# A new order of pieces in the third stage of a two-layer decoder

## The reference, cut to what matters

```
x = x + L0_attn(layernorm(x))            # linear attention with convolution and decay
x = x + L0_xattn(layernorm(x), ctx)      # a recurrence with w and u
x = x + L0_ffn(layernorm(x))             # 8 experts, top 2
x = x + L1_attn(layernorm(x))            # D: 16 heads of 16, 4 key heads, rotary, band and sink
x = x + L1_xattn(layernorm(x), ctx)      # E: per token, a 16 x 16 softmax between heads
x = x + L1_ffn(layernorm(x))             # F and M
```

```
mod  = 0.1 * tanh(attn @ A)                       # A: 256 x 16
gate = silu(h @ W_in.T + (mod * (h @ A)) @ B)     # B: 16 x 1024
out  = residual + (gate * (h @ W_up.T)) @ W_down.T
```

## Time and profile before

| | us |
|---|---|
| median of 3 runs (3017.0 to 3025.15) | 3019.28 |
| the profiled execution | 3016.38 |
| its span, first to last instruction | 3014.7 |
| busy PE / DVE / POOL / ACT in the span | 2755.2 / 2487.1 / 2099.5 / 1990.4 |
| the third stage's two costliest lines: POOL L1843 / L1836 | 370.1 / 359.2 |

### The profile page before, as it was taken

The page is one execution under the profiler, slowest core; times in us unless marked ns, Lnnn a source line. Parts: engine busy times, 40 slices in busy tenths (PEclk is TensorE's granted clock), DMA queues, the critical chain, the costliest instruction groups (busy, mean ns, idle before and its releaser), DMA issues. The chain is left out here.

```text
span 3014.7 us, 68300 instructions
## 1 busy us (share of the span) xinstructions
PE 2755.2 (91%) x22096; PEld 2297.8 (76%) x22128; DVE 2487.1 (83%) x5468; ACT 1990.4 (66%) x4233; POOL 2099.5 (70%) x2618
## 2 busy tenths in 40 slices
PE   6999999999999999999799499667899999999988
PEld 3888888888888888888555399535777777777767
DVE  6888888888888888888599677468889898989873
ACT  5888878878787887878576355345566666666642
POOL 6897666666666666666467544379898988898870
PEclk9999999999999999999899699768999999999999
DMA  4555444444434444444344499500000000000000
...
DMA packets 185883, 340.11 MB, mean 113 GB/s; under 512 B 40668, under 2 KB 104037, under 8 KB 178936
## 3 DMA queue, kind: packets, MB, share of 16 engines
...
...
## 5 line engine op out<-in xcount | busy, mean ns | idle before, releaser
L1843 POOL TENSOR_TENSOR l_prod<-l_sco,l_kv 128x256 f32<-128x256 f32 x512 | 370.1, 762 | 35.4 <-DVE l_sco L2350 35.4
L1836 POOL TENSOR_TENSOR l_prod<-l_q,l_kv 128x256 f32<-128x256 f32 x512 | 359.2, 741 | 45.7 <-DVE l_att L2358 45.7
L718 DVE SCALAR_TENSOR_TENSOR a_cq<-a_PQ,a_taps,a_cq 128x504 f32<-128x504 f32 (+2 forms) x384 | 281.9, 734 | 74.9 <-ACT a_cq L584 65.8
L718 DVE SCALAR_TENSOR_TENSOR a_ck<-a_PK,a_taps,a_ck 128x504 f32<-128x504 f32 (+2 forms) x384 | 280.8, 731 | 9.4 <-ACT a_ck L584 0.3
L342 POOL TENSOR_TENSOR a_tq<-a_cq,a_tq 128x512 f32<-128x512 f32 x128 | 166.0, 1297 | 130.7 <-ACT a_tq L590 130.3
L329 POOL TENSOR_TENSOR a_hrs<-a_hve,a_neghalf 128x8 f32<-128x8 f32 x128 | 209.7, 1638 | 25.3 <-DVE a_hve L735 25.3
L485 PE MATMUL a_Y<-a_wo,a_og_parts 128*128 128x256 f32 x1536 | 207.2, 285 | 4.5 <-POOL a_og_parts L336 4.5
L412 PEld LDWEIGHTS a_X<-a_wv,a_xb 128*128 128x128 f32 x1536 | 199.8, 188 | 12.1 <-issue 1.2
L412 PE MATMUL a_PQ<-a_x_hi,a_wqk 128*128 (+1 forms) x512 | 196.1, 424 | 12.6 <-issue 11.9
L342 POOL TENSOR_TENSOR a_tk<-a_ck,a_tk 128x512 f32<-128x512 f32 x128 | 163.6, 1278 | 62.8 <-ACT a_tk L590 62.8
L412 PE MATMUL a_X<-a_wv,a_xb 128*128 128x256 f32 x1536 | 204.1, 282 | 0.8 <-DMA a_xb<-a_x_lo 0.8
...
## 6 DMA issues: line engine op xcount, KB each, us to landing
...
a_dr<-decays SPq DMA_DIRECT2D x256, 64.0 KB, 2.5
...
```

Source lines behind the costliest of these rows:

```text
L718: nc.vector.scalar_tensor_tensor(out=acc, in0=src, scalar=taps[p][:, tap + k:tap + k + 1], in1=acc, op0=ALU.mult, op1=ALU.add).then_inc(s_ ...
L1836: nc.gpsimd.tensor_tensor(out=prod[:, h], in0=qv[:, h:h + 1, :].to_broadcast([P, H, HD]), in1=kk, op=ALU.mult).then_inc(S("E_pqk"), 1)
L1843: nc.gpsimd.tensor_tensor(out=prod[:, h], in0=sco[:, h:h + 1, :].to_broadcast([P, HD, H]), in1=vv, op=ALU.mult).then_inc(S("E_pav"), 1)
```

## The change

The pieces of all four engines stand in a new order. In each lap the PE list moves `ft_av` behind `d_qkT`, `d_s` ahead of `d_v`, and `f_v` to the end. The ACT list moves `m_tanh(0)` behind `et_exp`, `m_tanh(1)` ahead of the copy of E's queries, `f_x1` ahead of `f_x2`, and others. The DVE list moves `m_hidden(1)` ahead of `combine`, spreads the value sums in the order 0, 1, 2, 3, and puts `ft_gm_lo`, `arguments("D")`, `m_x`, `f_x2lo` ahead of `et_x`. POOL's list stays, but a group of four score products waits for one value sum more than the group before it, instead of all for all four; `gather` reads its offsets from `slots`; `of_tile`, `ready` and `gmT` are gone. `ft_gm` writes its rows over its input in the bank MI, and that bank is free for the next transpose when all three parts of `gm3` are written.

```diff
-                   ("ft_a", "Ft", [("F_gm", 1, 1)])],
+                   ("ft_a", "Ft", [("F_gm3", 3, 3)])],
...
             def products_qk(t):
-                wait_if(pool, S("E_att"), 4 * t)
                 for h in range(H):
+                    if t and h % 4 == 0:
+                        pool.wait_ge(S("E_att"), 4 * t - 3 + h // 4)
...
             def gather(t):
-                wait_if(pool, S("G_ready"), 2 * t)
                 wait_if(pool, S("G_x"), 2 * t)
-                nc.gpsimd.tensor_tensor(out=ready[:], in0=neghalf[:, 0:1], in1=neghalf[:, 0:1], op=ALU.mult).then_inc(S("G_ready"), 1)
-                nc.gpsimd.tensor_copy(of_tile[:], slots[:, tile(t), :].rearrange("p t k -> p (t k)")).then_inc(S("G_at"), 1)
-                pool.wait_ge(S("G_ready"), 2 * t + 1)
-                pool.wait_ge(S("G_at"), t + 1)
-                nc.gpsimd.tensor_tensor(out=ready[:], in0=neghalf[:, 0:1], in1=neghalf[:, 0:1], op=ALU.mult).then_inc(S("G_ready"), 1)
                 for k in range(2):
-                                                 bass.IndirectOffsetOnAxis(ap=of_tile[:, k:k + 1], axis=0)).then_inc(S(f"G_in{k}"), 16)
+                                                 bass.IndirectOffsetOnAxis(ap=slots[:, t, k:k + 1], axis=0)).then_inc(S(f"G_in{k}"), 16)
...
             iterate(pe, [("M", m_half(0)), ("D", d_xT), ("E", e_xT), ("Dt", d_eT), ("D", d_qk), ("Dt", d_av), ("Ft", ft_eT), ("E", e_q),
-                         ("F", f_zT), ("M", m_half(1)), ("Ft", ft_av), ("Dt", d_oT), ("D", d_qkT), ("Dt", d_wo), ("F", f_qk),
-                         ("Ft", ft_oT), ("D", d_v), ("F", f_v), ("Ft", ft_a), ("D", d_s), ("Md", m_down), ("Et", et_aT), ("Et", et_wo),
-                         ("F", f_s)])
+                         ("F", f_zT), ("M", m_half(1)), ("Dt", d_oT), ("D", d_qkT), ("Ft", ft_av), ("Dt", d_wo), ("F", f_qk),
+                         ("Ft", ft_oT), ("D", d_s), ("D", d_v), ("Ft", ft_a), ("Md", m_down), ("Et", et_aT), ("Et", et_wo),
+                         ("F", f_s), ("F", f_v)])
...
             def ft_gm_hi(t):
-                    nc.scalar.activation(gm3[t // 2 % 2][32 * k:32 * k + R, t % 2 * P:(t % 2 + 1) * P], gmT[:], ACT.Copy)
+                    nc.scalar.activation(gm3[t // 2 % 2][32 * k:32 * k + R, t % 2 * P:(t % 2 + 1) * P], MI[0:R, P:2 * P], ACT.Copy)
...
-            iterate(act, [("M", m_tanh(0)), ("D", leave(xT["D"], ...)), ("Dt", weights_T("D", "F", -4)),
-                          ("Ft", exponentials("F")), ("E", leave(xTE, ...)), ("Et", et_exp),
-                          ("F", normalise("F")), ("F", f_x2), ("F", f_x1), ("Ft", weights_T("F", "D", 5)), ("E", e_q), ("F", f_x2hi),
-                          ("M", m_tanh(1)), ("Dt", leave(oT["D"], ...)), ("D", spread_keys("D", P1, "D_qkTp")),
-                          ("D", queries("D", P1, ...)), ("Ft", leave(oT["F"], ...)),
-                          ("F", f_residual), ("F", spread_keys("F", P0, "F_pj")), ("Ft", ft_mod), ("D", d_vb), ("Ft", ft_gm_hi),
-                          ("En", normalise("E")), ("Et", leave(attT, ...)),
-                          ("F", queries("F", P0, ...)), ("Dn", normalise("D")), ("F", f_vb), ("Et", split_high),
-                          ("D", exponentials("D"))])
+            iterate(act, [("Et", split_high), ("Ft", exponentials("F")), ("D", leave(xT["D"], ...)),
+                          ("Dt", weights_T("D", "F", -4)), ("E", leave(xTE, ...)), ("Et", et_exp), ("M", m_tanh(0)),
+                          ("F", normalise("F")), ("F", f_x1), ("Ft", weights_T("F", "D", 5)), ("M", m_tanh(1)), ("E", e_q), ("F", f_x2),
+                          ("Dt", leave(oT["D"], ...)), ("F", f_residual), ("D", spread_keys("D", P1, "D_qkTp")),
+                          ("D", queries("D", P1, ...)), ("F", f_x2hi), ("F", queries("F", P0, ...)),
+                          ("Ft", leave(oT["F"], ...)), ("F", spread_keys("F", P0, "F_pj")), ("Ft", ft_mod), ("D", d_vb),
+                          ("Ft", ft_gm_hi), ("Et", leave(attT, ...)), ("En", normalise("E")), ("Dn", normalise("D")),
+                          ("D", exponentials("D")), ("F", f_vb)])
...
             def ft_gm(t):
-                wait_if(dve, S("F_gm3"), 3 * t)
                 dve.wait_ge(S("F_mod"), t + 1)
-                nc.vector.scalar_tensor_tensor(out=gmT[:], in0=MI[0:R, P:2 * P], scalar=MOD_SCALE, in1=modT[:], op0=ALU.mult,
+                nc.vector.scalar_tensor_tensor(out=MI[0:R, P:2 * P], in0=MI[0:R, P:2 * P], scalar=MOD_SCALE, in1=modT[:], op0=ALU.mult,
                                                op1=ALU.mult).then_inc(S("F_gm"), 1)
             def ft_gm_lo(t):
-                nc.vector.tensor_tensor(out=part[64:64 + R, :], in0=gmT[:], in1=part[0:R, :].bitcast(F32), op=ALU.subtract)
+                nc.vector.tensor_tensor(out=part[64:64 + R, :], in0=MI[0:R, P:2 * P], in1=part[0:R, :].bitcast(F32), op=ALU.subtract)
...
-            iterate(dve, [("Et", et_scores(0)), ("Ft", arguments("F")), ("F", statistics("F", "E_x", 1)), ("Et", et_scores(2)),
-                          ("Et", et_scores(1)), ("Et", et_scores(3)), ("Et", et_shift), ("Dt", divide("D", EB)), ("Et", et_weights),
-                          ("M", m_hidden(0)), ("D", d_rope), ("Dn", combine), ("Et", et_values(0)), ("Ft", divide("F", MI)),
-                          ("Dn", statistics("D", "G_x", 2)), ("F", f_x2lo), ("Dt", d_x), ("M", m_hidden(1)),
-                          ("En", statistics("E", "D_x", 1)), ("Et", et_values(2)), ("Et", et_values(1)), ("Ft", ft_gm),
-                          ("Et", et_values(3)), ("D", arguments("D")), ("Ft", ft_gm_lo), ("Md", m_x), ("Et", et_x), ("Et", split_low)])
+            iterate(dve, [("Et", et_scores(0)), ("F", statistics("F", "E_x", 1)), ("Ft", arguments("F")), ("Et", et_scores(2)), ("Et", et_scores(1)),
+                          ("Et", et_scores(3)), ("Et", et_shift), ("Dt", divide("D", EB)), ("Et", et_weights), ("M", m_hidden(0)), ("D", d_rope),
+                          ("Et", et_values(0)), ("M", m_hidden(1)), ("Dn", combine), ("Ft", divide("F", MI)), ("Et", split_low),
+                          ("Dn", statistics("D", "G_x", 2)), ("Dt", d_x), ("Et", et_values(1)), ("En", statistics("E", "D_x", 1)),
+                          ("Et", et_values(2)), ("Ft", ft_gm), ("Et", et_values(3)), ("Ft", ft_gm_lo), ("D", arguments("D")), ("Md", m_x),
+                          ("F", f_x2lo), ("Et", et_x)])
```

More of the change, by code:

```diff
@@ L1705, in layer_one @@
         got = [sb(f"got{k}", [P, D]) for k in range(2)]
-        of_tile, ready = sb("of_tile", [P, 2], mybir.dt.uint32), sb("ready", [P, 1])
         xT = {k: sb("xT" + k, [P, DC, P]) for k in "DF"}
@@ L1729, in layer_one @@
         att, attT = sb("att", [P, D]), sb("attT", [P, DC, P])
-        modT, gmT = sb("modT", [R, P]), sb("gmT", [R, P])
+        modT = sb("modT", [R, P])
         gm3 = [sb(f"gm3{k}", [3 * 32, 2 * P], F32R) for k in range(2)]
@@ L1768, in layer_one @@
         USES = {
-            "EB": [("d_xT", "D", [("D_xT", 1, 1)]), ("d_av", "Dt", [("D_o", 1, 1)]), ("e_q", "E", [("E_q", 1, 1)]),
-                   ("d_oT", "Dt", [("D_oT", 1, 1)]), ("d_wo", "Dt", [("D_x", 1, 1)]), ("d_v", "D", [("D_vb", 4, 4)]),
-                   ("et_aT", "Et", [("E_aT", 1, 1)]), ("et_wo", "Et", [("E_x", 1, 1)])],
+            "EB": [("d_xT", "D", [("D_xT", 1, 1)]), ("d_av", "Dt", [("D_o", 1, 1)]), ("e_q", "E", [("E_q", 1, 1)]), ("d_oT", "Dt", [("D_oT", 1, 1)]),
+                   ("d_wo", "Dt", [("D_x", 1, 1)]), ("d_v", "D", [("D_vb", 4, 4)]), ("et_aT", "Et", [("E_aT", 1, 1)]),
+                   ("et_wo", "Et", [("E_x", 1, 1)])],
             "SS": [("d_eT", "Dt", [("D_eT", 1, 1)]), ("ft_eT", "Ft", [("F_eT", 1, 1)]), ("d_s", "D", [("D_arg", 1, 1)]),
@@ L2079, in _ @@
             pe.wait_ge(S("woa"), 1)
-            iterate(pe, [("M", m_half(0)), ("D", d_xT), ("E", e_xT), ("Dt", d_eT), ("D", d_qk), ("Dt", d_av), ("Ft", ft_eT), ("E", e_q),
-                         ("F", f_zT), ("M", m_half(1)), ("Ft", ft_av), ("Dt", d_oT), ("D", d_qkT), ("Dt", d_wo), ("F", f_qk),
-                         ("Ft", ft_oT), ("D", d_v), ("F", f_v), ("Ft", ft_a), ("D", d_s), ("Md", m_down), ("Et", et_aT), ("Et", et_wo),
-                         ("F", f_s)])
+            iterate(pe, [("M", m_half(0)), ("D", d_xT), ("E", e_xT), ("Dt", d_eT), ("D", d_qk), ("Dt", d_av), ("Ft", ft_eT), ("E", e_q), ("F", f_zT),
+                         ("M", m_half(1)), ("Dt", d_oT), ("D", d_qkT), ("Ft", ft_av), ("Dt", d_wo), ("F", f_qk), ("Ft", ft_oT), ("D", d_s),
+                         ("D", d_v), ("Ft", ft_a), ("Md", m_down), ("Et", et_aT), ("Et", et_wo), ("F", f_s), ("F", f_v)])
         @block.scalar
@@ L2205, in ft_gm_hi @@
                 for k in range(2):
-                    nc.scalar.activation(gm3[t // 2 % 2][32 * k:32 * k + R, t % 2 * P:(t % 2 + 1) * P], gmT[:], ACT.Copy).then_inc(S("F_gm3"), 1)
+                    nc.scalar.activation(gm3[t // 2 % 2][32 * k:32 * k + R, t % 2 * P:(t % 2 + 1) * P], MI[0:R, P:2 * P],
```

(11 more changed lines are left out.)

6 lines of the change are left out of this document (removed).

## The result

The change made the kernel slower: 3185.3 us (median of 4 runs, 3173.4 to 3188.8) against 3018.1 us beside it, a ratio of 1.055 with an interval of 1.051 to 1.059. Forecast were 2986 us, with 3010 as the upper end. The profiled execution took 3173.4 us, its span is 3171.5.

What follows compares the result with a forecast made beforehand. A ring of waits between PE and DVE was taken to set the 30.02 us lap. 25 laps at 29.0 us give 25.5 us, the ends 1 + 4 + 3: 33.5 us less, 2986 us; range 2972 to 3010.

Steps and rivals of the forecast that it cites:

- ring B: New ring of waits through PE, ACT's copies and DVE's last pieces, `ft_gm_lo` to `et_x`: 29.04 us a lap.
- a lap above 29.7 us: Stated sign that the forecast is wrong, for laps between starts of the score products; 29.0 us was expected.
- the cover of what follows: POOL's lap falls to 27.2 us and its 1.25 us wait goes: worth nothing by itself in the 25 laps.
- rival 4: Gather issues from the whole offset table take 3.0 us each in place of 1.0; slower, 3045 us; chance 0.06.
- Rivals 2 and 3: ACT late in ring B, lap 29.6, 3003 us, chance 0.14; another hand-over absorbs the gain, 3010 to 3020, chance 0.06.
- The rings: Wait cycles between engines in the 25 middle laps: 28.8 us through `e_q` and `et_wo`, 29.04 through `ft_gm_lo`; lap 29.0.
- PE's own lap: PE's unchanged instructions without its waits at `e_q` and `d_wo`: 28.95 to 29.06 us a lap.
- The gather: On POOL, two small products and a copy go: 0.65 to 1.11 us less a lap, 0.7 taken.
- The ends: Laps around the middle 25: first two -1 us, next three -4, last two -3, drain 0.
- Moves costed at nothing: Reordered pieces counted as 0, such as ACT's order (up to 0.5 us) and `et_values(0)` right behind `d_rope` (0 to 0.2).

Runs made afterwards that it cites:

- run 3: Changed kernel with the first operand of `f_x2lo` read from PSUM bank EB in place of the copy x2f: 3006.7 us, ratio 0.995.
- run 13: Changed kernel with POOL's score products also waiting at the start for `ft_gm`, a short pause: 3001.4 us, ratio 0.995.
- Run 14: Kernel before with `f_x2lo` behind `m_x` and the changed kernel's score-product waits, so POOL doesn't pause: 3177.4 us, ratio 1.054.
- run 1: Changed kernel with `f_x2lo` alone put back ahead of `d_x`: 3008.7 us, ratio 0.996.
- run 8: Changed kernel with `f_x2lo`, `combine` and the two splits of the MLP's weights put back: 2987.7 us, ratio 0.991.
- 11: Changed kernel with `f_x2lo` and the two splits put back, `combine` left where the change puts it: 2990.6 us, ratio 0.990.
- run 4: Changed kernel with the score products waiting for all four value sums again: 3009.6 us, ratio 0.996.

## Why the prediction was wrong, point by point

**The step that failed** is in ring B: "`f_x2lo` 0.41". Its median measured 6.67 us. Its line over the 25 laps alone, in 23 of which it was shut out:

```profile
L2372 DVE TENSOR_TENSOR l_x<-l_x2f,l_x 128x256 fp32r<-128x256 f32 x25 | 152.9, 6117 | 0.0
```

The sum gave it 25 x 0.41 = 10.3 us, so this one term is short by 142.6 of the 166 us by which the 25 laps (891.2) miss the forecast (25 x 29.0 = 725). The low clock behind PE's new wait may make up the rest; no run takes that apart. The prediction's own sign of being wrong, a lap above 29.7 us, came with 35.65. The 0.41 came from the row at 2338.52, where `f_x2lo` stands beside value products; I took it for a property of the instruction. The Trainium skill's rule that I weighed for `ft_gm_lo` (SBUF — State Buffer, "Who interferes with whom"), two inputs in SBUF against GpSimd's reads, holds for `f_x2lo` just the same, as run 3 shows, and the change moved it; I applied it only where it promised a gain, at 0.3 us. Even the row at 2010.75, 16.05 us of products beside the splits, showed that such pairs can cost microseconds. By the Trainium skill (SBUF — State Buffer, "SBUF: two separate sides"), whichever of the two starts first gets the shared ports for its whole instruction and the other is blocked; by an estimate from that, one product (0.7 us) at most would have been the price. The trace agrees only in the kernels with a pause (0.84 us in run 13). Without one, 6.67 us is a wait over some ten products.

**Behind the step** lies that I counted the removal of POOL's 1.25 us wait as worth nothing, "the cover of what follows". That pause was what let DVE's instructions with two operands in SBUF in (runs 13 and 14). No rival had it: rival 4 was the only slower one, and its mechanism is refuted, as the gather's issues take 1.03 and 0.95 us from the table of slots. Rivals 2 and 3, with laps of 29.6 and about 30 us, are refuted by the 28.92 to 29.02 of run 1.

**The rings** were right once that is taken away. Forecast 29.0 us; 28.92 to 29.02 in run 1, 28.93 to 29.08 in run 13, whose timeline of POOL also shows the 1.8 us forecast before the value products:

```profile
2514.40 11.40 POOL L1845 TENSOR_TENSOR l_prod<-l_sco,l_kv 128x256 f32<-128x256 f32 x16 [1.78 <-DVE l_sco L2345]
```

The 25 laps gained 24.5 us in run 8, of 25.5.

**`ft_gm_lo`**: I kept 0.6 and named 0.28; it took 0.28 us in all 32 (281 to 283 ns). The lap didn't become 28.7 by it; PE's own lap, forecast at 28.95 to 29.06, is what fits the 28.95: over 20 laps of run 8 PE's only wait in the view is 0.6 us a lap at `et_wo`, for the copy of `attT` that the forecast left in PE's lap.

```profile
PE l_EB L1880 <- ACT l_attT L2085: 12.5, 20, 0.6
```

Run 14 shows what this edit is worth where POOL doesn't pause: without it `ft_gm_lo` is the one that is shut out.

**The gather** gives POOL 0.97 us a lap (0.14 us from the last product to the first issue, 1.11 before), against 0.7 taken.

**The ends** were wrong: -1, -4 and -3 us were forecast. In the changed kernel they are 22 us longer (17.2 and 4.9), with shut-outs of `f_x2lo` in them; in run 8, with `f_x2lo` back, 0 came. There the first two laps take 3.7 us more than in the earlier trace rows, the next three 2.4 less, the rest 0.9 less, and run 8 has the splits back in their old places. PE's low clock in those laps (0.58 and 0.85) would explain that removing POOL's wait helps little; I had named it, and still counted half of POOL's wait. No run tests it. The low end of the range also adds up wrong: the stated bounds of the ends sum to 3 + 7 + 5 + 2 = 17 us, not 13.

**Moves costed at nothing**: a price of `combine`'s new place can't be told from runs 8 and 11, whose ratios are 0.991 and 0.990; a shut-out of it, as in run 4, adds some 7 us to a lap.
